# One Trainium2 core, Mamba-like block plus ternary FFN: another order for VectorE and ScalarE around the last three tiles, and the last block's norm on VectorE

## The chip, the cores and the metric

The kernel runs on one core of one Trainium2 chip. The metric is the device time of one execution in microseconds (us). The kernel before takes 1438.84 us, the median of 3 runs (1438.45 to 1439.49).

## What is computed

The input is 8192 rows of 512 numbers (float32). Two sublayers follow each other, each `x = x + norm(f(norm(x)))`, with `norm` a layer norm without weights:

```
uv = x @ in_proj_w + in_proj_b;  u, v = halves of uv;  v = silu(v)
v  = depthwise conv of 3 taps along the rows + conv_b
h_t = a * h_{t-1} + ssm_b * v_t;  y = ssm_c * h + ssm_d * v        (scan along the rows)
h  = (u * silu(y)) @ out_proj_w + out_proj_b + x
attn = layernorm(h) * ln_w + ln_b
ffn  = gelu(x @ ternary(W1).T + b1) @ ternary(W2).T + b2           (inner width 2048)
```

## The kernel before

**Tiles and stages.** The rows are cut into 16 tiles (`NT = 16`, numbered 0 to 15) of 512 rows, and each tile into 4 blocks of 128 rows. Wide products are made of float16 halves ("high" and "low", `hi` and `lo`), three matmuls for each pair, so each result of TensorE needs a low half made by VectorE. A tile goes through: its `v` and `u` products (`in_proj`, L498 to L500, 12 matmuls for each of 4 groups), the scan, the gate (`gate`, L847: bias and product of a finished `u` bank with silu(y)), the split of the gated tensor (`gate_hi`, ScalarE L1542; `gate_lo`, VectorE L852), the output product (`o`, L511 to L513, 12 matmuls for each of 4 blocks), the addition of its result to the residual (`h_add`, VectorE L871), three layer norms (`norms`, L891 to L915, with `a1`, `a2`, `b_stats`, `x1`, `c_stats`, `n3`), the split of the FFN's input (`t_hi`, ScalarE L1566; `t_lo`, VectorE L860), its transposes by DMA, and the FFN: 16 times `f1` (8 matmuls, L531, L532), `gelu` and `hi` on ScalarE (L1478, L1488), `lo` on VectorE (L754) and `f2` (8 matmuls, L559, L560), at the end the scaling and bias of the four sums (`f_add`, L767).

**The pipeline.** A step `s` handles three tiles at once: the FFN of tile `s-2`, the first sublayer of tile `s-1` and the first product of tile `s+1`; the end of tile `s-3` (its last norm and sum) lies in it too. The last steps are special. Step 15 has the second part of the FFN of tile 13 (chunks 9 to 15), then the `u` products and the output product of tile 15 behind them, since there is no further tile to load. Step 16 is the FFN of tile 14 with the norms of tile 15 beside it, step 17 the FFN of tile 15 alone, and then come the last norm and sum of tile 15.

**What sets the order.** Each engine works through its own list in order, and waits on semaphores. The lists are written out by hand, or sorted from tables of places (`AT_...` at the top): `run(items)` (L84) sorts pairs of a number and a piece of work. The numbers are places in the list, not times. `AT_LO_LAST` holds the places of `lo` of chunks 9 to 15 in step 15, `AT_LO` those of step 16, `AT_GATE_LAST` those of the first two gates of tile 15, `AT_T3_LO` those of `t_lo`. The norms of step 15 stand at 7.7 and each 0.25 further, those of step 16 at 0.5 and on. GpSimd (POOL) makes every reciprocal standard deviation: an addition (`ve`, L1865) and a power (L1866), and VectorE's `a1`, `x1` and `n3` wait for them. GpSimd also adds the output bias to the residual of tile 15 (`add_bias`, L1918, four of them) and makes the last sum of every tile but the last (`finish`, L1908).

**Banks.** `u`, `v` and `o` products take turns on two PSUM banks, `misc0` and `misc1`, so a product waits for the reader of the one two places before it: `u` group 2 of tile 15 waits for gate 0, group 3 for gate 1, `o` block 0 for gate 2, block 1 for gate 3, block 2 for `h_add` 0 and block 3 for `h_add` 1. `o` also waits for each `gate_lo`, quarter by quarter (L509). The FFN's sums of tile 13 lie in four banks `f2b`; `f_add` empties them, and may write block `j` of `hb` once `t_lo` of tile 14 has read that block.

**The end.** For tile 15 VectorE makes `f_add`, the statistics and their aggregate block by block (L1460). GpSimd makes scale and shift (`rstd_last`, L1899: `ve`, power, product, negation) for blocks 0 and 1 together, then 2, then 3 (`FINAL`, L67). ScalarE norms each block (`ffn_norm`, L1499), VectorE adds the residual (L1466, the residual less its own shift was made earlier by `less_shift`), and SyncE stores the block.

```
            for j in range(NB):
                ve_.wait_ge(fn_ok, NB * e + j + 1)
                ve_.tensor_tensor(hb[:, j, :], hb[:, j, :], xs[:, e % X_SLOTS, j, :], ALU.add).then_inc(fin_last, 1)
```

Of the kernel before, what the change touches and what calls it, by code (L numbers as in the profile page):

```python
# [28 lines left out]
KC = D // P  # L29
# [34 lines left out]
AT_SILU_LAST, AT_GATE_LAST = 16.15, (15.0, 15.75)  # L64
AT_LO_LAST = (8.6, 9.6, 10.6, 11.65, 11.66, 12.2, 12.9)
AT_T3_HI_PAIR = (16.2, 16.4, 16.6, 16.8)
AT_XC = 13.3  # L67
FINAL = ((0, 2), (2, 3), (3, 4))
# [24 lines left out]
def build(nc, x, w_in, w_out, w1t, w2t, params, rows, out):  # L93
# [22 lines left out]
    with ExitStack() as ctx:  # L116
# [603 lines left out]
        def _(ve_):  # L720
# [207 lines left out]

            def add_bias(j):

                ve_.wait_ge(row_in, 16)
                ve_.wait_ge(x1_lo, j + 1)
                ve_.tensor_tensor(hb[:, j, :], hb[:, j, :], ob_row, ALU.add).then_inc(ob_ok, 1)
# [437 lines left out]
            for s in STEPS:  # L1371
# [17 lines left out]
                if fa is not None:  # L1389
                    items += [(AT_LO[j] if j < len(AT_LO) else 1.2 + j, lambda j=j: lo(fa, j))  # L1390
                              for j in range(half(s))]
# [21 lines left out]
                if s == NT - 1:  # L1413
                    for b in range(KC):
                        taps(NT - 1, b, False)
                    scan(NT - 1, 0)
                    scan(NT - 1, 1)
                items = []
                if c is not None:
                    for j in range(NB):  # L1420
                        h_add(c, j)
                        if s == NT - 1:
                            if j < 2:
                                scan(NT - 1, 2 + j)
                            y(NT - 1, j)
# [11 lines left out]
                if c is not None:  # L1437
                    items += [(at, lambda j=j: t_lo("t3", c, j)) for j, at in enumerate(AT_T3_LO)]
# [3 lines left out]
                if s == NT - 1:  # L1442
# [6 lines left out]
                    for j in range(NB):  # L1449
                        f_add(NT - 3, j)  # L1450
                    for j in range(NB):
                        f_stats(NT - 3, j)
                        h_add(NT - 1, j)
# [10 lines left out]
            for j in range(NB):  # L1464
                ve_.wait_ge(fn_ok, NB * e + j + 1)
                ve_.tensor_tensor(hb[:, j, :], hb[:, j, :], xs[:, e % X_SLOTS, j, :], ALU.add).then_inc(fin_last, 1)  # L1466
# [3 lines left out]
        def _(act):  # L1470
# [323 lines left out]
            for s in STEPS:  # L1794
# [45 lines left out]
                if s == NT - 1:  # L1840
                    items += [(AT_SILU_LAST, lambda b=b: silu_y(NT - 1, b)) for b in range(KC)]
                run(items)
                if s == NT - 1:
                    for b in range(KC):
                        gate_hi(NT - 1, b)
            for i, (j0, j1) in enumerate(FINAL):
# [6 lines left out]
        def _(pool):  # L1853
# [45 lines left out]
            def rstd_last(js):  # L1899

                pool.wait_ge(fn_ok, NB * (NT - 1))
                rstd(4, NT - 1, rs4[:, js], False, js)
# [179 lines left out]
```

## Time and profile before

| | |
|---|---|
| runs | 1438.84 us median of 3 (1438.45 to 1439.49) |
| the profiled execution | 1439.29 us, of which the span from the first to the last instruction is 1436.6 us |
| TensorE (PE) busy | 1405.8 us, 98% of the span |
| VectorE (DVE) busy | 1116.4 us, 78% |
| ScalarE (ACT) busy | 876.9 us, 61% |
| GpSimd (POOL) busy | 437.0 us, 30% |
| granted TensorE clock | 0.995 of full speed |

The profile is of one execution. The rows of its views name an engine, a line of the kernel, the operation and the tensors written and read; a bracket at the end of a row of the timeline tells how long the engine was idle before it and what ended that. The busy shares are those of the whole span. The change touches only its last 200 us, so what it is worth is read from the timeline of that stretch.

### The profile page before, as it was taken

The numbers are of one execution on the slowest core, as the hardware profiler recorded it, in microseconds if no ns is written. First come the engines' busy times: TensorE is split into PE (matmuls) and PEld (weight loads), VectorE is DVE, ScalarE is ACT, GpSimd is POOL, SyncE is SP. The second block draws the span as 40 slices with busy tenths as digits, with TensorE's granted clock in tenths as the row PEclk, the third lists the DMA queues.
The fourth block names the chain that finished last, engine by engine and source line by source line (L and its number), as shares of the span: only waits on it lengthen the run. The fifth ranks groups of instructions, "written<-read, shape, count | busy, mean of one in ns | idle before, by whom it ended". The sixth has DMA issues, their size and how long they took to land.

```text
span 1436.6 us, 19033 instructions
## 1 busy us (share of the span) xinstructions
PE 1405.8 (98%) x6528; PEld 641.9 (45%) x6528; DVE 1116.4 (78%) x1891; ACT 876.9 (61%) x1261; POOL 437.0 (30%) x520
## 2 busy tenths in 40 slices
PE   7998999999999999999999999999999999999997
PEld 5443444444444444444444444444444444443443
DVE  7999796867878677796867978677786877998634
ACT  7897665656756466565656756466565656753443
POOL 4325142320513225132330424214132331522221
PEclk9999999999999999999999999999999999999999
DMA  9713211221213113111221213113121221001200
GB/s 249 240 40 90 57 60 30 61 57 31 67 23 89 30 30 88 27 62 30 55 64 30 67 23 88 30 30 88 22 68 30 52 66 30 30 1 30 59 30 29
DMA packets 155984, 82.00 MB, mean 57 GB/s; under 512 B 132720, under 2 KB 132720, under 8 KB 155760
## 3 DMA queue, kind: packets, MB, share of 16 engines
q1 hardware_dynamic: 155888, 80.79, 22.0%
q8 instruction: 51, 0.84, 0.2%
q14 instruction: 45, 0.37, 0.1%
HBM read 31.49 MB, written 16.78 MB: 34 GB/s over the span
## 4 chain that ended last, share of the span: by engine, by line
PE 83%; DVE 4%; issue 2%; ACT 1%; POOL 1%; DMA 0%; DVEq 0%; POOLq 0%; ACTq 0%; SPq 0%
PE f1b L531 14%; PE f1b L532 14%; PE f2b L559 14%; PE f2b L560 14%; PE misc L498 6%; PE misc L500 6%; PE misc L499 6%; PE misc L511 3%; PE misc L513 3%; PE misc L512 3%; DVE bn L736 1%; DVE vl L812 0%; DVE yb L847 0%; DVE g_lo L852 0%; POOL rsc L1866 0%
## 5 line engine op out<-in xcount | busy, mean ns | idle before, releaser
L559 PE MATMUL f2b<-w,ring 128*128 128x512 fp8e5 x1008 | 382.1, 379 | 0.6 <-DVE ring L754 0.6
L560 PE MATMUL f2b<-w,ring 128*128 128x512 fp8e5 x1008 | 382.0, 379 | 0.0
L531 PE MATMUL f1b<-x3T,w 128*128 128x512 f16 x960 | 365.0, 380 | 2.3 <-DMA x3T<-tp 0.9
L532 PE MATMUL f1b<-x3T,w 128*128 128x512 f16 x960 | 365.0, 380 | 0.0
L1478 ACT ACTIVATE ring<-f1b,par 128x512 f32<-128x512 f32 x256 | 175.1, 684 | 238.9 <-PE f1b L532 238.5
L1865 POOL TENSOR_SCALAR ve<-mv 128x4 f32<-128x4 f32 (+2 forms) x88 | 33.6, 382 | 718.7 <-DVE mv L746 718.5
L754 DVE SCALAR_TENSOR_TENSOR ring<-ring,f_sc 128x512 f16<-128x512 f32 x256 | 208.7, 829 | 41.0 <-ACT ring L1488 41.0
L1488 ACT ACTIVATE ring<-ring,f_sc 128x512 f16<-128x512 f32 x256 | 180.0, 711 | 0.0
L498 PE MATMUL misc<-x1T,win_hi 128*128 128x512 f16 x464 | 175.9, 379 | 2.2 <-DVE yb L847 2.1
L500 PE MATMUL misc<-x1T,win_lo 128*128 128x512 f16 x464 | 175.9, 379 | 0.0
L499 PE MATMUL misc<-x1T,win_hi 128*128 128x512 f16 x464 | 175.9, 379 | 0.0
L559 PEld LDWEIGHTS f2b<-w,ring 128*128 128x128 f16 x1008 | 98.6, 98 | 120.4 <-DVE ring L754 1.9
L560 PEld LDWEIGHTS f2b<-w,ring 128*128 128x128 f16 x1008 | 98.6, 98 | 118.5
L531 PEld LDWEIGHTS f1b<-x3T,w 128*128 128x128 fp8e5 x960 | 94.1, 98 | 118.0 <-issue 4.9
L532 PEld LDWEIGHTS f1b<-x3T,w 128*128 128x128 fp8e5 x960 | 94.1, 98 | 113.4 <-issue 1.3
L1591 ACT ACTIVATE vb<-misc,par,inv_sig 128x512 f32<-128x512 f32 x54 | 41.8, 775 | 143.7 <-PE misc L500 143.6
L736 DVE BATCH_NORM_STATS2 bn<-hb 128x6 f32<-128x512 f32 x184 | 118.9, 679 | 0.2
L812 DVE SCALAR_TENSOR_TENSOR vl<-vb,par,vl 128x512 f32<-128x512 f32 x128 | 108.2, 883 | 1.8 <-ACT vl L1508 1.7
L1908 POOL TENSOR_TENSOR hb<-hb,xs 128x512 f32<-128x512 f32 x60 | 102.2, 1733 | 21.8 <-ACT hb L1499 21.8
L1918 POOL TENSOR_TENSOR hb<-hb,row 128x512 f32<-128x512 f32 x56 | 73.7, 1318 | 86.4 <-ACT hb L1529 86.4
L511 PE MATMUL misc<-wo_hi,g_hi 128*128 128x512 f16 x240 | 91.0, 379 | 4.9 <-DVE hb L871 2.8
L1913 POOL COPY carry<-vl 128x1 f32<-128x1 f32 x60 | 73.0, 1233 | 63.0 <-DVE vl L821 61.9
(211 smaller groups left out, 2043.1 us busy)
## 6 DMA issues: line engine op xcount, KB each, us to landing
out_dram<-hb SPq DMA_DIRECT2D x64, 256.0 KB, 2.0
xs<-x_dram SPq DMA_DIRECT2D x14, 1024.0 KB, 5.7
ring<-w1t_dram SPq DMA_DIRECT2D x3, 1024.0 KB, 12.3
stage<-w2t_dram SPq DMA_DIRECT2D x3, 1024.0 KB, 8.2
x1T<-tp SPq DMA_TRANSPOSE x68, 3.1
xs<-x_dram SPq DMA_DIRECT2D x4, 256.0 KB, 3.4
stage<-w_in_dram SPq DMA_DIRECT2D x4, 256.0 KB, 5.6
xs<-x_dram SPq DMA_DIRECT2D x2, 512.0 KB, 7.2
```

The lines of the kernel that those rows point to most:

```text
L498: pe.matmul(o[:, :], wh, x1T[:, s_, k, :], start=k == 0, stop=False)
L499: pe.matmul(o[:, :], wh, x1T[:, s_, KC + k, :], start=False, stop=False)
L500: mm = pe.matmul(o[:, :], wl, x1T[:, s_, k, :], start=False, stop=k == KC - 1)
L511: pe.matmul(out_[:, :], g_hi[:, k, js], wo_hi[:, k, :], start=k == 0, stop=False)
L531: pe.matmul(b[:, :], w, src[:, k, :], start=k == 0, stop=False)
L532: mm = pe.matmul(b[:, :], w, src[:, KC + k, :], start=False, stop=k == KC - 1)
L559: pe.matmul(f2b[q][:, :], h_hi[:, i % H_SLOTS, qs], w2[:, j, :], start=j == 0, stop=False)
L560: mm = pe.matmul(f2b[q][:, :], h_lo[:, i % H_SLOTS, qs], w2[:, j, :], start=False, stop=j == FC - 1)
L736: ve_.bn_stats(raw_stats(ln)[:, j, :], src).then_inc(bn_ok[ln], 1)
L754: ve_.scalar_tensor_tensor(out=h_lo[:, i % H_SLOTS, :], in0=gg[:, i % G_SLOTS, :], scalar=f_sc[:, 0:1], in1=h_hi[:, i % H_SLOTS, :], op0=A ...
L1478: act.activation(gg[:, i % G_SLOTS, :], f1b[i % 2][:, :], ACT.Gelu, bias=par[:, B1 + j:B1 + j + 1], scale=1.0 / ACT_SCALE).then_inc(gelu_o ...
L1488: act.activation(h_hi[:, i % H_SLOTS, :], gg[:, i % G_SLOTS, :], ACT.Copy, scale=f_sc[:, 0:1]).then_inc(hh_ok, 1)
```

## The change

- In step 15 the first `lo` (chunk 9) goes ahead of the four `a1`, and behind them no `lo` stands any more until the four `a2` are through.
- In step 15 scan 1 of tile 15 goes behind the first `h_add` of tile 14, scans 2 and 3 each one place later too.
- Gate 1 of tile 15 goes from behind the first two `t_lo` to right behind gate 0; `t_lo` of blocks 2 and 3 of tile 14 go behind the last `gate_lo`. ScalarE makes `gate_hi` 0 and 1 between `t_hi` 1 and 2.
- The first `h_add` of tile 15 goes between the second and third `f_add` of tile 13, the others one place forward among the statistics.
- In step 16 the places of the first eight `lo` are others (`AT_LO_PAIR`).
- The last block of tile 15 is normed by VectorE from mean and scale; ScalarE no longer does it, and GpSimd's product and negation for it are gone.

```diff
-AT_SILU_LAST, AT_GATE_LAST = 16.15, (15.0, 15.75)
-AT_LO_LAST = (8.6, 9.6, 10.6, 11.65, 11.66, 12.2, 12.9)
+AT_SILU_LAST, AT_GATE_LAST, AT_GATE_HI_LAST = 16.15, (15.0, 15.1), 16.5
+AT_LO_LAST = (7.65, 9.6, 10.6, 11.65, 11.66, 12.2, 12.9)
...
+AT_LO_PAIR = (0.45, 1.3, 1.9, 2.4, 3.4, 5.1, 6.0, 7.3)
...
+            def last_norm(j):
+
+                ve_.wait_ge(rs_ok[4], NT + len(FINAL) - 1)
+                ve_.tensor_scalar(hb[:, j, :], hb[:, j, :], mean_var(4)[:, j, 0:1], rs4[:, j:j + 1],
+                                  ALU.subtract, ALU.mult).then_inc(fn_ok, 1)
+
+            def last_sum(j):
+
+                ve_.wait_ge(fn_ok, NB * (NT - 1) + j + 1)
+                ve_.tensor_tensor(hb[:, j, :], hb[:, j, :], xs[:, (NT - 1) % X_SLOTS, j, :], ALU.add).then_inc(fin_last, 1)
...
-                    items += [(AT_LO[j] if j < len(AT_LO) else 1.2 + j, lambda j=j: lo(fa, j))
+                    at_lo = AT_LO_PAIR if s == NT else AT_LO
+                    items += [(at_lo[j] if j < len(at_lo) else 1.2 + j, lambda j=j: lo(fa, j))
...
                     scan(NT - 1, 0)
-                    scan(NT - 1, 1)
...
                         if s == NT - 1:
-                            if j < 2:
-                                scan(NT - 1, 2 + j)
+                            if j < NB - 1:
+                                scan(NT - 1, 1 + j)
                             y(NT - 1, j)
...
-                    items += [(at, lambda j=j: t_lo("t3", c, j)) for j, at in enumerate(AT_T3_LO)]
+                    items += [(at, lambda j=j: t_lo("t3", c, j)) for j, at in enumerate(AT_T3_LO) if s < NT - 1 or j < 2]
...
-                    for j in range(NB):
-                        f_add(NT - 3, j)
+                    t_lo("t3", NT - 2, 2)
+                    t_lo("t3", NT - 2, 3)
+                    f_add(NT - 3, 0)
+                    f_add(NT - 3, 1)
+                    h_add(NT - 1, 0)
+                    f_add(NT - 3, 2)
+                    f_add(NT - 3, 3)
                     for j in range(NB):
                         f_stats(NT - 3, j)
-                        h_add(NT - 1, j)
+                        if j < NB - 1:
+                            h_add(NT - 1, j + 1)
                         h_stats(NT - 1, j)
                         aggr(4, NT - 3, j)
...
-            for j in range(NB):
-                ve_.wait_ge(fn_ok, NB * e + j + 1)
-                ve_.tensor_tensor(hb[:, j, :], hb[:, j, :], xs[:, e % X_SLOTS, j, :], ALU.add).then_inc(fin_last, 1)
+            for j in range(NB - 1):
+                last_sum(j)
+            last_norm(NB - 1)
+            last_sum(NB - 1)
...
                     items += [(AT_SILU_LAST, lambda b=b: silu_y(NT - 1, b)) for b in range(KC)]
+                    items += [(AT_GATE_HI_LAST, lambda b=b: gate_hi(NT - 1, b)) for b in range(2)]
                 run(items)
                 if s == NT - 1:
-                    for b in range(KC):
+                    for b in range(2, KC):
                         gate_hi(NT - 1, b)
-            for i, (j0, j1) in enumerate(FINAL):
+            for i, (j0, j1) in enumerate(FINAL[:-1]):
...
                 pool.wait_ge(fn_ok, NB * (NT - 1))
+                if js.stop == NB:
+                    rstd(4, NT - 1, rs4[:, js], True, js)
+                    return
```

Three pieces of VectorE's list show what moved, as lines with the operation and its tensors; a line of the changed kernel has a number higher by one. The first is the beginning of the norms of tile 14 in step 15. L891 is `a1`, L896 `a2`, and the write to `ring` is `lo` of chunks 9 and 10. Before:

```order
L746 BN_AGGR mv<-bn 128x2 x2
L891 SCALAR_TENSOR_TENSOR hb<-hb,mv,row 128x512 x4
L754 SCALAR_TENSOR_TENSOR ring<-ring,f_sc 128x512
L896 SCALAR_TENSOR_TENSOR hb<-hb,rsc,row 128x512 x4
L754 SCALAR_TENSOR_TENSOR ring<-ring,f_sc 128x512
```

Now:

```order
L747 BN_AGGR mv<-bn 128x2 x2
L755 SCALAR_TENSOR_TENSOR ring<-ring,f_sc 128x512
L892 SCALAR_TENSOR_TENSOR hb<-hb,mv,row 128x512 x4
L897 SCALAR_TENSOR_TENSOR hb<-hb,rsc,row 128x512 x4
L755 SCALAR_TENSOR_TENSOR ring<-ring,f_sc 128x512
```

`lo` of chunk 9 went from behind the `a1` to ahead of them, and nothing stands between `a1` and `a2`.

The second piece is the end of these norms. `hb<-xs,mv,rsc` is `n3`, `yb<-misc...` a gate, `tp<-hb,tp` is `t_lo` and `g_lo` is `gate_lo`. Before:

```order
L915 TENSOR_SCALAR hb<-xs,mv,rsc 128x512 x2
L847 SCALAR_TENSOR_TENSOR yb<-misc0,bu_sig,yb 128x512
L915 TENSOR_SCALAR hb<-xs,mv,rsc 128x512
L860 SCALAR_TENSOR_TENSOR tp<-hb,tp 128x512
L915 TENSOR_SCALAR hb<-xs,mv,rsc 128x512
L860 SCALAR_TENSOR_TENSOR tp<-hb,tp 128x512
L847 SCALAR_TENSOR_TENSOR yb<-misc1,bu_sig,yb 128x512
L860 SCALAR_TENSOR_TENSOR tp<-hb,tp 128x512 x2
L852 SCALAR_TENSOR_TENSOR g_lo<-yb,g_sc,g_hi 128x512
L847 SCALAR_TENSOR_TENSOR yb<-misc0,bu_sig,yb 128x512
```

Now:

```order
L916 TENSOR_SCALAR hb<-xs,mv,rsc 128x512 x2
L848 SCALAR_TENSOR_TENSOR yb<-misc0,bu_sig,yb 128x512
L848 SCALAR_TENSOR_TENSOR yb<-misc1,bu_sig,yb 128x512
L916 TENSOR_SCALAR hb<-xs,mv,rsc 128x512
L861 SCALAR_TENSOR_TENSOR tp<-hb,tp 128x512
L916 TENSOR_SCALAR hb<-xs,mv,rsc 128x512
L861 SCALAR_TENSOR_TENSOR tp<-hb,tp 128x512
L853 SCALAR_TENSOR_TENSOR g_lo<-yb,g_sc,g_hi 128x512
L848 SCALAR_TENSOR_TENSOR yb<-misc0,bu_sig,yb 128x512
```

Gate 1 (the first on `misc1`) has moved over an `n3` and a `t_lo` and more, and the last two `t_lo` are gone from ahead of the first `gate_lo`.

The third piece follows it: `hb<-f2b...` is `f_add` of tile 13 and `xs<-misc...` is `h_add` of tile 15. Before:

```order
L852 SCALAR_TENSOR_TENSOR g_lo<-yb,g_sc,g_hi 128x512
L847 SCALAR_TENSOR_TENSOR yb<-misc1,bu_sig,yb 128x512
L852 SCALAR_TENSOR_TENSOR g_lo<-yb,g_sc,g_hi 128x512 x2
L767 SCALAR_TENSOR_TENSOR hb<-f2b0,f_inv,row 128x512
L767 SCALAR_TENSOR_TENSOR hb<-f2b1,f_inv,row 128x512
L767 SCALAR_TENSOR_TENSOR hb<-f2b2,f_inv,row 128x512
L767 SCALAR_TENSOR_TENSOR hb<-f2b3,f_inv,row 128x512
L736 BN_STATS bn<-hb 128x6
L871 SCALAR_TENSOR_TENSOR xs<-misc0,o_inv,xs 128x512
```

Now:

```order
L853 SCALAR_TENSOR_TENSOR g_lo<-yb,g_sc,g_hi 128x512
L848 SCALAR_TENSOR_TENSOR yb<-misc1,bu_sig,yb 128x512
L853 SCALAR_TENSOR_TENSOR g_lo<-yb,g_sc,g_hi 128x512 x2
L861 SCALAR_TENSOR_TENSOR tp<-hb,tp 128x512 x2
L768 SCALAR_TENSOR_TENSOR hb<-f2b0,f_inv,row 128x512
L768 SCALAR_TENSOR_TENSOR hb<-f2b1,f_inv,row 128x512
L872 SCALAR_TENSOR_TENSOR xs<-misc0,o_inv,xs 128x512
```

The two `t_lo` stand here now, behind all four `gate_lo`, and `h_add` 0 has gone ahead of two `f_add` and a `bn_stats`.

## Rows read from the trace of the kernel before

**Rows 1.** The page: busy time, share of the span, instructions of each engine

```profile
PE 1405.8 (98%) x6528; PEld 641.9 (45%) x6528; DVE 1116.4 (78%) x1891; ACT 876.9 (61%) x1261; POOL 437.0 (30%) x520
```

**Rows 2.** Timeline of TensorE, end of step 15: start us, us, row, [idle <-what ended it]

```profile
1263.84 0.39 PE L511 MATMUL misc<-wo_hi,g_hi 128*128 128x512 f16 x1 [0.20 <-DVE hb L871]
...
1278.40 0.39 PE L559 MATMUL f2b<-w,ring 128*128 128x512 fp8e5 x1 [0.58 <-DVE ring L754]
...
1298.91 0.38 PE L500 MATMUL misc<-x1T,win_lo 128*128 128x512 f16 x1
...
1303.45 0.39 PE L498 MATMUL misc<-x1T,win_hi 128*128 128x512 f16 x1 [1.39 <-DVE yb L847]
...
1308.84 0.39 PE L511 MATMUL misc<-wo_hi,g_hi 128*128 128x512 f16 x1
...
1312.72 0.39 PE L511 MATMUL misc<-wo_hi,g_hi 128*128 128x512 f16 x1 [0.48 <-DVE xs L871]
```

**Rows 3.** Timeline of VectorE, scans, additions and norms of tile 14, step 15

```profile
1261.88 1.25 DVE L821 TENSOR_TENSOR_SCAN vl<-a_par,carry,vl 128x512 f32<-128x512 f32 x1
1263.06 0.72 DVE L871 SCALAR_TENSOR_TENSOR hb<-misc,o_inv,hb 128x512 f32<-128x512 f32 x1
...
1274.94 2.74 DVE L891 SCALAR_TENSOR_TENSOR hb<-hb,mv,row 128x512 f32<-128x512 f32 x4 [1.47 <-POOL rsc L1866]
1277.60 0.74 DVE L754 SCALAR_TENSOR_TENSOR ring<-ring,f_sc 128x512 f16<-128x512 f32 x1
...
1284.90 1.38 DVE L754 SCALAR_TENSOR_TENSOR ring<-ring,f_sc 128x512 f16<-128x512 f32 x2
...
1291.41 0.73 DVE L754 SCALAR_TENSOR_TENSOR ring<-ring,f_sc 128x512 f16<-128x512 f32 x1
```

**Rows 4.** Timeline of GpSimd, step 15: powers for the norms, last bias addition

```profile
1273.87 1.04 POOL L1866 TENSOR_TENSOR rsc<-ve,mhalf 128x4 f32<-128x4 f32 x1
...
1285.79 1.39 POOL L1866 TENSOR_TENSOR rsc<-ve,mhalf 128x4 f32<-128x4 f32 x1
...
1299.67 1.45 POOL L1918 TENSOR_TENSOR xs<-xs,row 128x512 f32<-128x512 f32 x1
```

**Rows 5.** Timeline of VectorE, end of step 15: n3, t_lo and the first f_add

```profile
1295.68 2.89 DVE L915 TENSOR_SCALAR hb<-xs,mv,rsc 128x512 f32<-128x512 f32 x2 [1.47 <-POOL rsc L1866]
...
1299.91 1.75 DVE L860 SCALAR_TENSOR_TENSOR tp<-hb,tp 128x512 f16<-128x512 f32 x1
...
1303.31 1.28 DVE L860 SCALAR_TENSOR_TENSOR tp<-hb,tp 128x512 f16<-128x512 f32 x2
...
1308.69 2.72 DVE L767 SCALAR_TENSOR_TENSOR hb<-f2b,f_inv,row 128x512 f32<-128x512 f32 x4
```

**Rows 6.** Timeline of ScalarE, the last high half of the gated tensor

```profile
1307.27 0.72 ACT L1542 ACTIVATE g_hi<-yb,g_sc 128x512 f16<-128x512 f32 x1 [0.60 <-DVE yb L847]
```

**Rows 7.** Timeline of VectorE and TensorE, step 16: x1, lo and f2 of chunk 5

```profile
1338.58 2.74 DVE L906 SCALAR_TENSOR_TENSOR xs<-xs,rsc 128x512 f32<-128x512 f32 x4 [3.68 <-POOL c L1889]
...
1343.02 0.74 DVE L754 SCALAR_TENSOR_TENSOR ring<-ring,f_sc 128x512 f16<-128x512 f32 x1
...
1343.60 0.38 PE L532 MATMUL f1b<-x1T,w 128*128 128x512 f16 x1
1343.82 0.39 PE L559 MATMUL f2b<-w,ring 128*128 128x512 fp8e5 x1
```

**Rows 8.** Timeline of the end: VectorE, ScalarE, GpSimd

```profile
1430.25 1.88 DVE L1466 TENSOR_TENSOR hb<-hb,xs 128x512 f32<-128x512 f32 x3
1433.43 0.69 DVE L1466 TENSOR_TENSOR hb<-hb,xs 128x512 f32<-128x512 f32 x1 [1.30 <-ACT hb L1499]
...
1432.59 0.81 ACT L1499 ACTIVATE hb<-hb,nm,rs 128x512 f32<-128x512 f32 x1 [1.48 <-POOL nm L1904]
...
1431.08 0.88 POOL L1866 TENSOR_TENSOR rs<-ve,mhalf 128x1 f32<-128x1 f32 x1
```

**Rows 9.** n3 on tile 15 with GpSimd idle (line L915): ns min/median/max

```profile
L915 DVE TENSOR_SCALAR xs<-xs,mv,rsc x4: 539/540/546, 1346.8 to 1348.8; 128x512 f32<-128x512 f32 x4
```

## The prediction

> **What bounds the kernel now.** The page first [rows 1]: TensorE is busy 98% of the span, the next engine 78%. So outside the start and the end only what makes TensorE wait can be won back. The timeline of TensorE in the stretch that the change touches comes second [rows 2]. A matmul is modelled as 0.38 us long, but the next starts 0.22 us after it (the two TensorE rows of [rows 7]), so a wait costs its bracket and 0.16 us more. The reader is to see four larger ones: 0.36 us before 1263.84 (for `h_add` of tile 14), 0.74 before 1278.40 (for `lo` of chunk 9), 1.55 before 1303.45 (for gate 1 of tile 15) and 0.64 before 1312.72 (for `h_add` 0 of tile 15). All four end on VectorE. The third view is VectorE's own timeline there [rows 3, 5], for what stands ahead of the piece that TensorE wants. The last is the end [rows 8]: after the sums of the last block GpSimd makes the power, a product and a negation, ScalarE norms, VectorE adds.
>
> What is won in step 15 stays won only if nothing later pins TensorE at a fixed time, so each step is followed to the next wait.
>
> **Scans (step 15).** Scan 1 starts at 1261.88 and `h_add` 0 follows it at 1263.06 [rows 3]. Now `h_add` 0 takes the earlier place, 1.18 us before, and the 0.36 us go. VectorE's own total is unchanged: its norms still start when they did.
>
> **First `lo` ahead of `a1`.** Before, VectorE is idle for 1.47 us ahead of the `a1` [rows 3], waiting for the power, which runs 1273.87 to 1274.91 [rows 4]. `lo` of chunk 9 (about 0.66 us from start to start: `a1` four times take 1274.94 to 1277.60) moves into that idle time. TensorE's wait of 0.74 us goes. VectorE would gain 0.66 us for all that follows, if `lo` in the gap cost the power nothing. Rows 4 speak against that: the second power has two `lo` beside it (the row at 1284.90 of [rows 3]) and takes 1.39 instead of 1.04 us, 0.35 more. One `lo` beside `ve` and power can cost nothing at best, and at worst its whole 0.66 us. I take 0.40, near the only row that shows such an overlap. The norms then run 0.26 us earlier (bounds 0 and 0.66).
>
> TensorE has by then won 0.36 + 0.74 = 1.10 us, but gets no further than VectorE: `lo` of chunk 10 stands behind all four `a2`, and `lo` of chunk 15 ends at 1292.14 [rows 3], where TensorE takes it up with hardly any wait before. Both run 0.26 us earlier, so here TensorE's gain shrinks from 1.10 to 0.26 us. **Most of the first two waits comes back as waits for `lo` 10 and `lo` 15.**
>
> **Gates and `t_lo`.** The two first `n3` start at 1295.42 (1295.68 less 0.26) and end after 2.89 us [rows 5], at 1298.31; gate 0 follows. Gate 1 needs `u` group 1, whose last matmul started at 1298.91 [rows 2]; 0.26 earlier and 0.42 for its end gives 1299.07. It ends at 1299.8, and TensorE, which starts group 2 at about 1299.0 and needs 12 matmuls of 0.216 us for it, reaches group 3 at 1301.6 without a wait: the 1.55 us go.
>
> Then VectorE: the third `n3` comes at 1299.7, during GpSimd's last addition, which now runs 1299.4 to 1300.9 (1299.67 and 1.45 us, less 0.26 [rows 4]). In the trace before, a `t_lo` that starts during that addition takes 1.75 us and ends 0.54 us behind it [rows 4, 5]; so I let the `n3` end at 1301.2. Behind it, by 0.6 for a `t_lo` (two take 1.28, the first's end lying under the second [rows 5]), 0.46 for an `n3` and 0.66 for gates and `gate_lo`: `t_lo` 0, `n3` 3, `t_lo` 1 until 1302.8; `gate_lo` 0 at 1302.8, gate 2 at 1303.46, `gate_lo` 1 at 1304.12, gate 3 at 1304.78, `gate_lo` 2 at 1305.44. Gate 3 ends at 1305.52; ScalarE's high half takes 0.72 [rows 6] and ends at 1306.28; `gate_lo` 3 runs 1306.32 to 1307.06, and TensorE starts the last quarter of `o` block 0 at 1307.12, where it was 1308.84 [rows 2]: **1.72 us earlier**. It still waits ahead of the last two quarters, about as long as before, since 1.2 us of `t_lo` are out of the way but TensorE is there sooner too.
>
> `h_add` 0: `gate_lo` 3, two `t_lo` (1.2) and two `f_add` (1.32, by four in 2.64) give its start at 1309.5 and its end at 1310.24. TensorE, with 15 more matmuls from 1307.12, needs it at 1310.36. So the 0.64 us go too, and TensorE enters step 16 **2.36 us earlier**. `h_add` 1 ends at 1312.8, needed at 1312.95: just in time.
>
> `f_add` 2 and 3 end later than the first two but are wanted only by `f2` of tile 14, five `f1` after the start of step 16: nothing. `t_lo` 2 and 3 end at 1308.2, their transposes are wanted 7 us later: nothing.
>
> **Step 16.** TensorE had no waits here and is now 2.36 us earlier at every chunk, and the new places answer that. The tightest is `lo` 5: it ended at 1343.76 and was wanted at 1343.82 [rows 7]. In its new place, behind three `x1`, it ends 2.0 + 0.75 us behind the start of the first. That start hangs on GpSimd, whose additions follow TensorE's time, so 1338.58 becomes 1336.2 and `lo` 5 ends at 1339.0; wanted at 1341.46. Nothing lost, so the 2.36 us reach the end.
>
> **The last block.** The power ends at 1431.96; from there a product, a negation, ScalarE's 0.81 us and 0.69 us of addition end at 1434.12 [rows 8]. Now VectorE norms itself: free after its three additions at about 1432.05 (start 1430.25, 0.60 each), 0.54 us for `n3`'s form with GpSimd idle [rows 9], then the addition from 1432.62. That replaces 1433.43: **0.81 us**. Bounds: 0.3 if this form took as long as ScalarE's 0.81 and the wait between the two were longer than between VectorE's others, 0.9 if VectorE were free at the power's end.
>
> **Sum.** 2.36 + 0.81 = 3.17 us off the profiled execution (1439.29, span 1436.6): 1436.1, span 1433.4. That execution is 0.45 us above the median of the runs. The median is forecast at 1438.84 - 3.17 = 1435.7 us. A measurement of this kernel can tell about 0.2%, 2.9 us, from no change, so the forecast lies 0.3 us beyond that line.
>
> **The rivals.**
> 1. *GpSimd has the port when `lo` 9 starts.* `lo` 9 starts at about 1273.64, while GpSimd is in the addition ahead of the power. If it blocks, or the power is pushed back by all of it, VectorE has nothing for all that follows: 2.36 - 0.26 + 0.81 = 2.91 us, 1435.9. For it: `t_lo` of 1.75 us [rows 5]. Against it: the power with two `lo` beside it lost only 0.35 us. The Trainium skill (SBUF — State Buffer, Who interferes with whom) says that whichever of VectorE with two SBUF inputs and GpSimd issues first holds the shared pair for its whole instruction and the other fully blocks; that is this rival, its sum would be 1435.9. By that rule the `t_lo` of 1.75 us agrees, and the power's 0.35 us, less than one `lo`, does not quite.
> 2. *No contention at all:* the norms run 0.66 earlier, 2.76 + 0.81 = 3.57 us, 1435.3. For it: one small instruction of GpSimd may slip by.
> 3. *TensorE finds a new wait:* `h_add` 1 has 0.15 us to spare, `h_add` 0 has 0.12, the quarters of `o` wait on VectorE in any case. If VectorE loses 1 us more (say that `n3` and `t_lo` both wait out GpSimd's additions), all of it shows: 2.17 us or less in all, 1436.7. With the last block's norm worth only 0.3 as well, 1.66 us, 1437.2.
> 4. *Slower: `lo` 5 is pinned behind `x1`.* `x1` waits for GpSimd, busy with four additions beside a VectorE without pause; 3.68 us of idle ahead of it [rows 7] show that this wait is real. `lo` 5 has 2.5 us to spare. Each us beyond costs TensorE one; at 5.6 us later the gain is gone, and from 8.5 us the kernel is slower by 0.2%: at 10 us, 1443.1. Against it: nothing added to GpSimd's work there.
>
> **Chances.** Forecast 0.45, rival 1 0.21, rival 2 0.13, rival 3 0.18, rival 4 0.03. The forecast and rival 1 lie near the line of 2.9 us (1435.96), so with a spread of the median of some 0.3 us I count three quarters of the first (0.34) and half of the second (0.11) as beyond it, and all of rival 2: 0.58 faster, 0.39 the same, 0.03 slower. The range takes in rivals 1 to 3 with their bounds and that spread: 1434.8 to 1437.2.
>
> **What would show it.** After: no bracket ahead of `u` group 3; the first `lo` inside VectorE's idle time ahead of `a1`, with the second part of that idle time telling whether the power grew; a wait of TensorE for `lo` 10 (`f2`), new; the last quarter of `o` block 0 about 1.7 us earlier; no wait for `h_add`; no waits in steps 16 and 17; the last addition 0.57 us behind VectorE's norm. The forecast is wrong if TensorE enters step 16 less than 2 or more than 2.8 us earlier, or if steps 16 and 17 have waits.

## The result and the profile after

The changed kernel takes 1436.07 us (median of 20 runs, 1433.88 to 1439.53), the kernel before beside it on the same chip 1438.53 us (20 runs, 1437.32 to 1442.02). The ratio is 0.9981, 95% interval 0.9975 to 0.9988: 2.7 us gone, 1.7 to 3.6 by the interval. The forecast was 1435.7 us and 3.17 us. The effect is real, since the interval leaves out no change. But its middle, 2.7 us, lies just short of the 2.9 us (0.2%) beyond which the prediction had put 0.58 of its chances.

The profiled execution of after has a span of 1436.6 us, the same as before's. It must not be read as "nothing gained". Two rows show why: the first `u` matmul of tile 14, the start of step 15. Everything ahead of it is unchanged code.

Timeline of TensorE, kernel before (start us, us, engine line op out<-in count [idle <-what ended it], so in all timelines below):

```profile
1241.02 0.38 PE L498 MATMUL misc<-x1T,win_hi 128*128 128x512 f16 x1
```

The same place, kernel after (its lines are numbered one higher here):

```profile
1243.76 0.38 PE L499 MATMUL misc<-x1T,win_hi 128*128 128x512 f16 x1
```

This execution reached step 15 2.74 us later. Single executions of one kernel lie 2 us and more to each side of their median, so neither spans nor single times settle an effect of 2.7 us. What repeats to some 0.02 us is the waits of TensorE inside one trace. So I use this measure: over all matmuls from 1225 us on, the sum of (start to start less 0.216 us) wherever the distance is over 0.25 us. It is 4.30 us in before and 2.36 in after: 1.94 us won. (The sums are of unrounded starts; those of printed rows can be 0.02 off.) The rest is the end: from the start of the last matmul to the end of the last addition 5.90 us before, 5.09 after, so 0.81 us. Together 2.75 us, which agrees with the ratio.

Page, after, busy time of each engine ([rows 1] of before):

```profile
PE 1406.8 (98%) x6528; PEld 641.7 (45%) x6528; DVE 1119.3 (78%) x1892; ACT 876.6 (61%) x1260; POOL 435.3 (30%) x518
```

VectorE has one instruction more, and 2.9 us more busy time, most of which is no work, as its rows in step 16 below show.

Timeline of TensorE, after, its six waits ([rows 2]; subtract 2.74 us to compare starts; the bracket leaves out 0.16 us, and waits below it have none):

```profile
1284.16 0.39 PE L560 MATMUL f2b<-w,ring 128*128 128x512 fp8e5 x1 [0.53 <-DVE ring L755]
...
1294.64 0.39 PE L560 MATMUL f2b<-w,ring 128*128 128x512 fp8e5 x1
...
1301.74 0.39 PE L499 MATMUL misc<-x1T,win_hi 128*128 128x512 f16 x1
...
1308.68 0.39 PE L512 MATMUL misc<-wo_hi,g_hi 128*128 128x512 f16 x1 [0.30 <-DVE g_lo L853]
...
1309.56 0.39 PE L512 MATMUL misc<-wo_hi,g_hi 128*128 128x512 f16 x1
...
1344.59 0.39 PE L560 MATMUL f2b<-w,ring 128*128 128x512 fp8e5 x1 [0.53 <-DVE ring L755]
```

In order: 0.69 us for `lo` 10 and 0.11 for `lo` 15 (new), 0.18 for gate 0, 0.45 and 0.22 for the last two `gate_lo` (0.60 and 0.23 before), and 0.69 for `lo` 5 of step 16 (new). The waits for `h_add`, `lo` 9 and gate 1 of [rows 2] are gone. Before step 16 the sum is 1.66 us, so TensorE entered it 4.30 - 1.66 = 2.64 us earlier. In step 16 it gave 0.69 back.

Timeline of VectorE and GpSimd, after, step 15, around `lo` 9 ([rows 3, 4]):

```profile
1276.37 0.75 DVE L755 SCALAR_TENSOR_TENSOR ring<-ring,f_sc 128x512 f16<-128x512 f32 x1
1278.05 2.74 DVE L892 SCALAR_TENSOR_TENSOR hb<-hb,mv,row 128x512 f32<-128x512 f32 x4 [0.93 <-POOL rsc L1886]
...
1276.63 1.39 POOL L1886 TENSOR_TENSOR rsc<-ve,mhalf 128x4 f32<-128x4 f32 x1
```

`lo` 9 lies in the idle time, and the power beside it takes 1.39 us instead of 1.04: `a1` starts 0.35 us later than it could. The forecast had taken 0.40.

Timeline of VectorE and GpSimd, after, step 16 (L897 is `a2`, L755 `lo`, L907 `x1`; L1931 are the four additions of `finish`):

```profile
1328.60 2.42 DVE L897 SCALAR_TENSOR_TENSOR xs<-xs,rsc,row 128x512 f32<-128x512 f32 x2
1330.95 1.75 DVE L755 SCALAR_TENSOR_TENSOR ring<-ring,f_sc 128x512 f16<-128x512 f32 x1
1332.62 3.43 DVE L897 SCALAR_TENSOR_TENSOR xs<-xs,rsc,row 128x512 f32<-128x512 f32 x2
1335.98 0.74 DVE L755 SCALAR_TENSOR_TENSOR ring<-ring,f_sc 128x512 f16<-128x512 f32 x1
...
1341.79 2.08 DVE L907 SCALAR_TENSOR_TENSOR xs<-xs,rsc 128x512 f32<-128x512 f32 x3 [1.75 <-POOL c L1909]
1343.79 0.74 DVE L755 SCALAR_TENSOR_TENSOR ring<-ring,f_sc 128x512 f16<-128x512 f32 x1
...
1328.90 3.25 POOL L1931 TENSOR_TENSOR hb<-hb,xs 128x512 f32<-128x512 f32 x2 [3.65 <-ACT hb L1518]
1332.36 3.15 POOL L1931 TENSOR_TENSOR hb<-hb,xs 128x512 f32<-128x512 f32 x2 [0.20 <-ACT hb L1518]
1340.13 0.23 POOL L1885 TENSOR_SCALAR ve<-mv 128x4 f32<-128x4 f32 x1 [4.62 <-DVE mv L747]
```

Two engines alternate here. The second `a2` starts 0.67 us behind the first, at 1329.27, and from there to 1335.98 VectorE issues four instructions in 6.71 us, 1.68 each instead of 0.66: 4.1 us lost, one for each addition of GpSimd. The `x1` then start at 1341.79, and `lo` 5 behind three of them ends 0.69 us late. Note the last row: GpSimd is idle for 4.62 us and waits for VectorE, not the other way round.

Before, the same four additions cost VectorE nothing. Timeline of GpSimd and VectorE, before, the first addition and what VectorE did beside it, and in the last row GpSimd's first instruction behind the fourth addition:

```profile
1328.83 3.88 POOL L1908 TENSOR_TENSOR hb<-hb,xs 128x512 f32<-128x512 f32 x1 [5.33 <-ACT hb L1499]
...
1328.84 0.75 DVE L754 SCALAR_TENSOR_TENSOR ring<-ring,f_sc 128x512 f16<-128x512 f32 x1
1329.50 0.75 DVE L896 SCALAR_TENSOR_TENSOR xs<-xs,rsc,row 128x512 f32<-128x512 f32 x1
1330.16 1.41 DVE L754 SCALAR_TENSOR_TENSOR ring<-ring,f_sc 128x512 f16<-128x512 f32 x2
1331.49 2.47 DVE L736 BATCH_NORM_STATS2 bn<-xs 128x6 f32<-128x512 f32 x4
...
1336.92 0.23 POOL L1865 TENSOR_SCALAR ve<-mv 128x4 f32<-128x4 f32 x1
```

Here GpSimd was held for 3.88 us, to 1.13 us behind the end of the last of VectorE's instructions with two SBUF inputs (1331.57), and VectorE kept its pace. The last row is the `ve` that `x1` waits for: it starts as the fourth addition ends, so in before `x1` hung on GpSimd's additions, as the prediction says, and in after on VectorE's statistics. GpSimd's bias additions of the same shape take 1.32 us in the mean. The lines view of GpSimd, before (op count | busy, mean ns | idle ahead):

```profile
L1918 POOL TENSOR_TENSOR hb<-hb,row 128x512 f32<-128x512 f32 x56 | 73.7, 1318 | 86.4 <-ACT hb L1529 86.4
```

The meeting itself had moved. Timeline of VectorE, before, the first three `a1` of step 16:

```profile
1323.53 2.08 DVE L891 SCALAR_TENSOR_TENSOR xs<-xs,mv,row 128x512 f32<-128x512 f32 x3 [3.59 <-POOL rsc L1866]
```

Timeline of GpSimd and VectorE, after, ahead of `a1` in step 16:

```profile
1323.17 0.65 POOL L1917 TENSOR_SCALAR nm<-tmp 128x4 f32<-128x4 f32 x1
...
1322.97 0.75 DVE L755 SCALAR_TENSOR_TENSOR ring<-ring,f_sc 128x512 f16<-128x512 f32 x1 [1.70 <-ACT ring L1507]
1325.28 1.42 DVE L892 SCALAR_TENSOR_TENSOR xs<-xs,mv,row 128x512 f32<-128x512 f32 x2 [1.56 <-POOL rsc L1886]
```

`a1` started at 1323.53 in before and at 1325.28 - 2.74 = 1322.54 in after: only 0.99 us earlier, since the statistics behind the last `f_add` were ready only 1.4 us earlier and one small GpSimd instruction took 0.65 us beside a `lo`, where it took 0.24 in before. The additions follow TensorE: 1328.90 - 2.74 = 1326.16, 2.67 us earlier. So they fall 1.7 us sooner into VectorE's norms.

Timeline of the end, after ([rows 8]; L933 is the norm, L939 the addition, L1886 the power):

```profile
1431.02 1.87 DVE L939 TENSOR_TENSOR hb<-hb,xs 128x512 f32<-128x512 f32 x3
1432.81 0.54 DVE L933 TENSOR_SCALAR hb<-hb,mv,rs 128x512 f32<-128x512 f32 x1
1433.39 0.69 DVE L939 TENSOR_TENSOR hb<-hb,xs 128x512 f32<-128x512 f32 x1
...
1431.85 0.88 POOL L1886 TENSOR_TENSOR rs<-ve,mhalf 128x1 f32<-128x1 f32 x1
```

Product, negation and ScalarE's pass are gone; the addition follows the norm by 0.58 us.

### The profile page after: what moved, and what is told of

Read it like the earlier page. It is cut to its first block, busy times and chain, and to the rows that moved or that the text cites. A ratio compares the mean times of both kernels' runs of the same rounds, so it can differ in the third digit from the quotient of the medians.

```text
span 1436.6 us, 19031 instructions
## 1 busy us (share of the span) xinstructions
PE 1406.8 (98%) x6528; PEld 641.7 (45%) x6528; DVE 1119.3 (78%) x1892; ACT 876.6 (61%) x1260; POOL 435.3 (30%) x518
## 4 chain that ended last, share of the span: by engine, by line
PE 77%; DVE 7%; issue 4%; ACT 1%; POOL 1%; DMA 1%; SPq 0%; DVEq 0%; ACTq 0%; POOLq 0%
PE f1b L532 13%; PE f2b L560 13%; PE f1b L533 13%; PE f2b L561 13%; PE misc L499 6%; PE misc L501 6%; PE misc L500 6%; PE misc L512 3%; PE misc L514 3%; PE misc L513 3%; DVE bn L737 1%; POOL rsc L1886 1%; DMA x3T<-tp 1%; DVE ring L755 1%; DVE hb L892 1%
## 5 line engine op out<-in xcount | busy, mean ns | idle before, releaser
L755 DVE SCALAR_TENSOR_TENSOR ring<-ring,f_sc 128x512 f16<-128x512 f32 x256 | 208.4, 827 | 40.8 <-ACT ring L1507 40.7
L1931 POOL TENSOR_TENSOR hb<-hb,xs 128x512 f32<-128x512 f32 x60 | 100.7, 1707 | 20.7 <-ACT hb L1518 20.7
```

The source lines that it names most:

```text
L755: ve_.scalar_tensor_tensor(out=h_lo[:, i % H_SLOTS, :], in0=gg[:, i % G_SLOTS, :], scalar=f_sc[:, 0:1], in1=h_hi[:, i % H_SLOTS, :], op0=A ...
```

## The experiments

Two theories stood after the result. **A:** the wait for `lo` 5 comes from the contention of VectorE and GpSimd in step 16, the alternation above. **B:** it comes from the new place of `lo` 5 alone. Beside them each part of the change was to be priced by itself. "Waits" is the measure above (before 4.30, after 2.36 us). Where a kernel was timed only once, its time is given beside that of the kernel before, but the waits decide. A short diff is against the changed kernel, unless it says otherwise.

### The end alone, and the changed kernel again

The first is the kernel before with `last_norm` and `last_sum`, and GpSimd's and ScalarE's parts of the last block left out. The second is unchanged.

```diff
# e1_end_only, against before
-            for j in range(NB):
-                ve_.wait_ge(fn_ok, NB * e + j + 1)
-                ve_.tensor_tensor(hb[:, j, :], hb[:, j, :], ...)
+            for j in range(NB - 1):
+                last_sum(j)
+            last_norm(NB - 1)
+            last_sum(NB - 1)
```

> The kernel before with the last block normed by VectorE and nothing else. If the term of the last block is right: from the start of the last matmul to the end of the last addition 5.90 us before, now 5.09 us (0.81 less), with the norm of 0.54 us starting when VectorE's third addition is through; TensorE's waits after 1240 us stay at 4.29 us in all. Rival (ScalarE's hand-over was hidden): 5.6 us or more.

> The changed kernel again. In its first profile TensorE waits 0.69 us for lo 5 of step 16, because four VectorE instructions of the norms there took 1.75 us instead of 0.75 beside GpSimd's additions (4.1 us lost). If that is how this order always meets GpSimd: the same four long instructions, TensorE's waits after 1240 us 2.3 to 2.4 us. If it is a matter of chance who gets there first: in this run VectorE's instructions are short, GpSimd's first addition takes 3 us or more, no wait for lo 5, 1.65 us in all.

The end alone: waits 4.31, last matmul to end 5.09 instead of 5.90 (one time, 1436.93, beside 1438.24). So the last part is worth 0.81 us by itself, and the two parts add. GpSimd's first addition in step 16 takes 3.88 us in this run too. The changed kernel again (1436.17 beside 1438.24): waits 2.35, among them 0.68 for `lo` 5, and the alternation is there to the hundredth.

VectorE, changed kernel again, step 16:

```profile
1326.06 2.42 DVE L897 SCALAR_TENSOR_TENSOR xs<-xs,rsc,row 128x512 f32<-128x512 f32 x2
1328.40 1.75 DVE L755 SCALAR_TENSOR_TENSOR ring<-ring,f_sc 128x512 f16<-128x512 f32 x1
1330.08 3.43 DVE L897 SCALAR_TENSOR_TENSOR xs<-xs,rsc,row 128x512 f32<-128x512 f32 x2
```

So which engine gives way is no chance of one execution; it repeats with the order. The alternation of the additions stands in every run with the changed places of step 16 and the additions ahead of the norms' work.

### `lo` 5 ahead of `x1`

```diff
-AT_LO_PAIR = (0.45, 1.3, 1.9, 2.4, 3.4, 5.1, 6.0, 7.3)
+AT_LO_PAIR = (0.45, 1.3, 1.9, 2.4, 3.4, 4.4, 6.0, 7.3)
```

> The changed kernel with lo 5 of step 16 ahead of x1 (4.4 instead of 5.1), into VectorE's idle time. Theory: the wait of 0.69 us for it goes, TensorE's waits after 1240 us 1.65 us, and the kernel is 3.4 us faster than before (ratio 0.9976); lo 6 then ends within 0.1 us of its need. Rival (lo 6 and 7 are as late, the wait only moves to the next chunk): waits stay at 2.3 us.

Waits 1.74: `lo` 5 is waited for no more, 0.07 us come back for `lo` 6. The alternation stays (2.42, 1.75, 3.43 us). Timed: 1436.66 us (11 runs) beside 1438.24 (15), ratio 0.999 (0.998 to 0.9999); too wide to show 0.6 us. Both theories allow this one: the place turns the loss of VectorE into a wait of TensorE.

### The additions of `finish` behind GpSimd's norm work

```diff
-                if e is not None:
+                if e is not None and s != NT:
                     items += [(0, lambda j=j: finish(e, j)) for j in range(NB)]
...
                     rstd(3, c, rsc[:, 2, :], True)
+                if s == NT:
+                    for j in range(NB):
+                        finish(e, j)
```

> The changed kernel with GpSimd's four additions for tile 13 moved behind its work for the norms of tile 15. Theory: the four VectorE instructions of 1.75 us in step 16 take 0.75 again, everything from the a2 on is 4.1 us earlier, lo 5 is in time, TensorE's waits after 1240 us are 1.65 us. Rival (something else holds x1): the wait of 0.69 us stays.

Timeline of VectorE in this run, step 16:

```profile
1324.41 1.41 DVE L897 SCALAR_TENSOR_TENSOR xs<-xs,rsc,row 128x512 f32<-128x512 f32 x2
1325.73 0.74 DVE L755 SCALAR_TENSOR_TENSOR ring<-ring,f_sc 128x512 f16<-128x512 f32 x1
1326.40 1.40 DVE L897 SCALAR_TENSOR_TENSOR xs<-xs,rsc,row 128x512 f32<-128x512 f32 x2
...
1342.14 5.70 DVE L916 TENSOR_SCALAR xs<-xs,mv,rsc 128x512 f32<-128x512 f32 x4 [1.24 <-POOL rsc L1886]
```

`lo` 5 kept its place behind `x1`, and its wait is gone: waits 1.67 (1435.33 beside 1438.11). That decides for A: the place costs nothing if VectorE isn't slowed. The contention moved to the four `n3`, 5.70 us, where four of 0.54 us [rows 9] would take 2.2 at most; nobody waits for them.

### The old places of `lo` in step 16

```diff
-                    at_lo = AT_LO_PAIR if s == NT else AT_LO
+                    at_lo = AT_LO
```

> The changed kernel with the old places of lo in step 16. Theory: TensorE, 2.6 us earlier than in the kernel before, outruns them: it waits about 1 us for lo 0 (behind three a1), and for lo 5 (behind all x1 and three statistics) 1 us or more; waits after 1240 us 3.5 us or more. Rival (the places buy nothing, only the contention of VectorE and GpSimd decides): 2.4 us as in the changed kernel.

Waits 5.04 us: 1.11 for `lo` 0, 1.79 for `lo` 1, 0.45 for `lo` 5 (1441.22 beside 1438.11). TensorE enters the step 2.64 us earlier than in before, `a1` starts only 1.4 us earlier (0.99 in after, where a `lo` stands beside GpSimd's chain), and a `lo` that stood in time behind it is now late. VectorE gives way to the additions here too (single instructions of 1.75 us), so it is not the new order of `lo` alone that turned the contest. The table of places is what keeps the gain of step 15: 2.68 us of it, the largest single price measured here. Without it the waits are longer than the 4.30 us of before.

### `lo` 9 back behind `a1`

```diff
-AT_LO_LAST = (7.65, 9.6, 10.6, 11.65, 11.66, 12.2, 12.9)
+AT_LO_LAST = (8.6, 9.6, 10.6, 11.65, 11.66, 12.2, 12.9)
```

> The changed kernel with lo 9 of step 15 behind the a1 again. Theory (lo 9 beside GpSimd's power costs 0.35 and frees 0.66): the power takes 1.04 instead of 1.39 us, the a1 start 0.35 us earlier against the aggregates, but everything from the a2 on is 0.31 us later; TensorE waits about 1.1 us for lo 9, nothing for lo 10, and enters step 16 0.3 us later than the changed kernel. Rival (no cost, 0.66 freed): 0.66 us later. Rival (all given back): at the same time.

Waits 2.68, 0.32 more (1439.39 beside 1438.24). TensorE waits 1.14 us for `lo` 9, but not for `lo` 10 (0.69) nor `lo` 15 (0.11). The power takes 1.04 us again. So most of this wait had only changed its name, as forecast.

### Gate 1 back

```diff
-AT_SILU_LAST, AT_GATE_LAST, AT_GATE_HI_LAST = 16.15, (15.0, 15.1), 16.5
+AT_SILU_LAST, AT_GATE_LAST, AT_GATE_HI_LAST = 16.15, (15.0, 15.75), 16.5
```

> The changed kernel with gate 1 of tile 15 back behind two n3 and two t_lo. Theory: TensorE waits 1.5 us for it again, the last quarter of o block 0 starts 1.6 us later than in the changed kernel; as TensorE then comes later to lo 5, that wait goes: waits after 1240 us 3.2 to 4.0 us. Rival (VectorE's total up to the last gate_lo decides, gate 1's place is worth little): 2.4 to 2.8 us.

Waits 3.89: 1.54 for gate 1 again, all else as in after (1435.89 beside 1438.11). The wait for `lo` 5 stayed at 0.70, although TensorE was 1.54 us later; I had thought that it might go. The additions and the norms follow TensorE, so all of them moved together. The gate is the change's main gain, and worth its whole wait.

### Scan 1 back ahead of `h_add` 0

```diff
                     scan(NT - 1, 0)
+                    scan(NT - 1, 1)
...
-                            if j < NB - 1:
-                                scan(NT - 1, 1 + j)
+                            if j < 2:
+                                scan(NT - 1, 2 + j)
```

> The changed kernel with scan 1 ahead of the first h_add of tile 14, as before. Theory (what the scan frees comes back as a wait for lo 10): the wait of 0.37 us for h_add returns and that for lo 10 shrinks from 0.69 to 0.32, the sum stays 2.36 us. Rival (the scan's gain is real): 2.7 us.

A miss, and the most useful run. Waits 1.99 (1436.95 beside 1438.11): *less* than the changed kernel's 2.36. The 0.37 us for `h_add` are back, but the 0.69 for `lo` 10 are gone. Timeline of VectorE and GpSimd, this run:

```profile
1275.33 0.75 DVE L755 SCALAR_TENSOR_TENSOR ring<-ring,f_sc 128x512 f16<-128x512 f32 x1 [0.53 <-ACT ring L1508]
1276.27 2.74 DVE L892 SCALAR_TENSOR_TENSOR hb<-hb,mv,row 128x512 f32<-128x512 f32 x4 [0.19 <-POOL rsc L1887]
...
1275.20 1.04 POOL L1887 TENSOR_TENSOR rsc<-ve,mhalf 128x4 f32<-128x4 f32 x1
```

TensorE is 0.37 us later here, so ScalarE gives `lo` 9 its input later. It starts 0.13 us *behind* the power and slows nothing; in after it starts 0.26 us *ahead* of it and costs it 0.35. `a1` is then 0.36 us earlier against the norms and TensorE 0.37 later: together 0.73, enough for the 0.69.

The Trainium skill (SBUF — State Buffer, Who interferes with whom) says that of a VectorE instruction with two SBUF inputs and a GpSimd instruction that reads SBUF the one that issues first holds the shared port pair and the other fully blocks. In the pair of runs here the order of the starts does decide, as it says. In after `lo` still had 0.49 us to run when the power began, and the power lost 0.35. But in e8 the power began first and neither blocked, which the rule does not give.

### Both: scan back, additions late

```diff
# e9_scan_back_finish_late: the two edits above together
```

> The changed kernel with two things of the runs before: scan 1 ahead of the first h_add again, and GpSimd's additions for tile 13 behind its work for the norms of tile 15. If the two are independent: TensorE's waits after 1240 us 1.99 - 0.69 = 1.30 us, the end 5.09 us behind the last matmul, together 3.8 us less than the kernel before, ratio 0.9973. Rival (what one frees meets the next wait): 1.7 to 2 us.

Waits 1.32 against 1.30 expected: the two causes are independent. Timed: 1435.15 us (12 runs) beside 1439.21 (23), ratio 0.9976 (0.9965 to 0.9987).

### Gates between the `n3`, `o` blocks interleaved

```diff
# against e9, VectorE
+                    late_n3[0]()
+                    gate(NT - 1, 0)
+                    late_n3[1]()
+                    gate(NT - 1, 1)
                     gate_lo(NT - 1, 0)
...
                     gate_lo(NT - 1, 3)
+                    late_n3[2]()
+                    t_lo("t3", NT - 2, 0)
+                    late_n3[3]()
+                    h_add(NT - 1, 0)
+                    t_lo("t3", NT - 2, 1)
...
+                    h_add(NT - 1, 1)
+                    for j in range(NB):
+                        f_add(NT - 3, j)
...
# TensorE
+                    o_part(first, 0, range(KC - 1))
+                    o_part(second, 1, range(1))
+                    o_part(first, 0, range(KC - 1, KC))
+                    o_part(second, 1, range(1, KC))
```

ScalarE makes its four high halves of the gate before the last two of `x3`.

> The same, and at the end of step 15 VectorE makes only two n3 ahead of the gates (gate 0 between them), the other n3 and all t_lo behind the last gate_lo, and TensorE makes the last quarter of o block 0 behind the first of block 1. Theory: the waits for gate 0 (0.17) and for the last two gate_lo (0.46 and 0.22) go, the chain gate 3, high half, gate_lo 3 of 2.5 us lying beside 12 matmuls now; waits after 1240 us 0.5 us, 4.6 us less than before, ratio 0.9968. Rival (h_add 0 and 1, now behind n3 and t_lo, are late): 1 us or more.

A miss. Waits 1.84, timed 1436.32 (11 runs) beside 1439.21 (23), ratio 0.9981 (0.9972 to 0.999). Timeline of TensorE and of SP's queue, this run:

```profile
1305.77 0.39 PE L522 MATMUL misc<-wo_hi,g_hi 128*128 128x512 f16 x1 [0.28 <-DVE g_lo L870]
...
1315.80 0.38 PE L543 MATMUL f1b<-x1T,w 128*128 128x512 f16 x1 [0.79 <-DMA x1T<-tp]
...
1307.73 5.99 SPq L405 DMA_TRANSPOSE x1T<-tp  x4
```

The gates' waits shrank from 0.85 to 0.44 us, but all of `t_lo` came behind them, the transposes with it, and `f1` of step 16 waited 0.95 us for the last. The prediction's "wanted 7 us later: nothing" for the transposes held for the change, but it left out that SP issues them one after the other: the four take 5.99 us together, of which 0.43 is a wait for a `t_lo`. With the last `t_lo` 2.2 us later than in after, the margin is gone.

### The same, with `n3` and `t_lo` spread between the gates

```diff
# against e10, VectorE
                     gate_lo(NT - 1, 0)
+                    late_n3[2]()
                     gate(NT - 1, 2)
                     gate_lo(NT - 1, 1)
-                    gate(NT - 1, 3)
+                    t_lo("t3", NT - 2, 0)
                     gate_lo(NT - 1, 2)
+                    gate(NT - 1, 3)
+                    t_lo("t3", NT - 2, 1)
                     gate_lo(NT - 1, 3)
-                    late_n3[2]()
-                    t_lo("t3", NT - 2, 0)
                     late_n3[3]()
-                    h_add(NT - 1, 0)
-                    t_lo("t3", NT - 2, 1)
                     t_lo("t3", NT - 2, 2)
+                    h_add(NT - 1, 0)
```

ScalarE's third high half of `x3` moves ahead of its third one of the gate.

> The run before showed two waits: 0.44 us for gate_lo 2, which stood behind gate 3 on VectorE, and 0.95 us for the transposes of tile 14, whose last t_lo ended at 1310.6. Now gate_lo 2 goes ahead of gate 3, and the n3 and t_lo fill VectorE's idle time between the gates. Theory: both waits go, what is left is 0.37 + 0.07, TensorE's waits after 1240 us 0.45 to 0.65 us, ratio to the kernel before 0.9968. Rival (a gate or gate_lo is pushed back by what was put ahead of it): 0.9 us or more.

Waits 0.78: 0.37 for `h_add`, 0.07 for `lo` 15, and 0.35 for `lo` 1 of step 16, the next to be late (below). Between `lo` 15 and step 16 there is no wait left. Timed: 1435.15 us (9 runs) beside 1438.63 (13), ratio 0.9975 (0.9965 to 0.9985).

Timeline of TensorE, VectorE and GpSimd, this run:

```profile
1326.35 0.39 PE L571 MATMUL f2b<-w,ring 128*128 128x512 fp8e5 x1 [0.18 <-DVE ring L772]
...
1322.89 2.74 DVE L909 SCALAR_TENSOR_TENSOR xs<-xs,mv,row 128x512 f32<-128x512 f32 x4 [3.24 <-POOL rsc L1912]
1325.55 0.74 DVE L772 SCALAR_TENSOR_TENSOR ring<-ring,f_sc 128x512 f16<-128x512 f32 x1
...
1318.89 0.75 DVE L772 SCALAR_TENSOR_TENSOR ring<-ring,f_sc 128x512 f16<-128x512 f32 x1
...
1319.14 1.41 POOL L1912 TENSOR_TENSOR rs<-ve,mhalf 128x4 f32<-128x4 f32 x1
```

Here `lo` 1 stands behind four `a1`, as `lo` 10 stands behind the four `a2` in after. The last two rows show `lo` 0 once more 0.25 us ahead of a power of the chain that `a1` waits for, and the power at 1.41 us instead of 1.04; that loss is as large as the wait, but no run tried `lo` 0 at another place. By the waits this is the best version, 1.58 us under the changed kernel; by time it can't be told from the e9 kernel, and it was not timed beside the changed kernel itself. Both beat the kernel before with their intervals.

## Why the prediction was right, and where it was not

| term | forecast, us | measured, us | from |
|---|---|---|---|
| TensorE enters step 16 earlier | 2.36 | 2.64 | waits 4.30 and 1.66 |
| step 16 | nothing lost | 0.69 lost | new wait for `lo` 5 |
| last block | 0.81 | 0.81 | 5.90 and 5.09 |
| sum | 3.17 | 2.76 (2.75 unrounded) | ratio: 2.7 |

**Scans.** The wait for `h_add` went, 0.37 us. In the forecast's sum this was worth nothing, since it lies in the 1.10 us that shrink to 0.26. That it cost nothing either was wrong: the run with the scan back shows that it brought `lo` 9 ahead of the power and cost more than it gave (1.99 against 2.36 us). The prediction priced the two parts of the change one by one and did not carry the 0.37 us of TensorE on to the start of `lo` 9.

**First `lo` ahead of `a1`.** Right in mechanism and size: power 0.35 us longer (taken 0.40), norms 0.3 earlier (0.26), the first two waits back as waits for `lo` 10 and 15 (0.69 and 0.11 seen). The run with `lo` 9 back confirms it. Rivals 1 and 2, the norms no earlier or a whole 0.66 us earlier, are both excluded for this kernel. Rival 1 had priced a block at the whole `lo`; 0.49 us of it were left when the power began.

**Gates and `t_lo`.** Right: gate 1's wait gone, priced at 1.54 us by the run with it back. The last quarter of `o` block 0 started at 1309.56, less 2.74 that is 1306.82: 2.02 us earlier, where 1.72 was forecast. Of the 0.30 us 0.27 are VectorE's third `n3`: it ended at 1300.93 on before's clock, not 1301.2, since GpSimd's four bias additions were done 0.26 us sooner. No wait for `h_add` 0 or 1.

Timeline of VectorE and GpSimd, after, the third `n3` and the bias additions ([rows 4, 5]):

```profile
1302.50 1.17 DVE L916 TENSOR_SCALAR hb<-xs,mv,rsc 128x512 f32<-128x512 f32 x1
...
1298.06 5.32 POOL L1941 TENSOR_TENSOR xs<-xs,row 128x512 f32<-128x512 f32 x4
```

The additions end at 1303.38, less 2.74 that is 1300.64, where the forecast had 1300.9.

**Step 16: the step that failed.** "Nothing lost" rested on two sentences: that GpSimd's additions follow TensorE's time, so that the `x1` start at 1336.2, and that `lo` 5 had 2.5 us to spare. The additions did follow. But the `x1` started at 1341.79, less 2.74 that is 1339.05: not 2.4 us earlier than before but 0.5 later, and 2.85 later than forecast. VectorE lost 4.1 us to the additions, and `x1` waited for its statistics, no longer for GpSimd: on before's clock the additions ended 4.2 us earlier than in before. The 2.85 us less `lo` 5's spare time, 2.46, which TensorE's extra 0.28 cut to 2.18, are 0.67; 0.69 was measured. The trace of before has an addition of 3.88 us there, three times the usual; that row was not read, and it was the sign that two engines contend there. What VectorE loses when it is the one that gives way stood in the prediction's own rows: two `n3` in 2.89 us and a `t_lo` of 1.75 beside the bias additions [rows 5]. It was counted in step 15 and left out in step 16. Rival 4 named the right instruction and the right pin but the wrong holder (a busy GpSimd); the delay was 2.85 us, far from the 8.5 at which it would have decided.

**Last block.** Right to 0.01 us, in the change and alone.

So the time fell into the range because a loss of 0.69 us and a gain of 0.28 both were smaller than the rivals allowed for. That 0.28 us of the loss were made up in step 15 is luck. By the prediction's own sign, waits in steps 16 and 17, its account of step 16 was wrong. What stays open: why GpSimd is shut out in before and alternates in after. It was not tried in isolation.

## What to carry to other kernels

When a step is moved earlier, follow its own timing to each place where VectorE and GpSimd overlap, and read the longest instance of a GpSimd instruction, not its mean: one that is three times its usual length marked, here, a contest that a shift of 1.7 us turned. An earlier TensorE is worth only what the vector work in the next stage can follow, so the places of that work belong to the change (here 2.68 us of it). Where runs scatter by more than the effect, sum TensorE's waits within one trace and undo each part of the change by itself: a part that removes a wait can still cost time.

## What the runs showed of the hardware

- Four GpSimd additions of 128x512 beside VectorE's instructions with two SBUF inputs went in two ways, each the same in every run of the same order. In before and in the kernel with only the end changed, the first was held for 3.88 us while VectorE kept 0.66 us per instruction. In the changed kernel both runs show strict alternation, VectorE at 1.68 us per instruction and GpSimd at 1.6 per addition. The 3.88 us stand alone: of the 120 GpSimd instructions of 128x512 with two inputs in before, the next longest took 2.29 us.
- In the alternation each engine waits for the other in full, up to a hand-over. An addition that found VectorE in such an instruction ended 1.13 us behind the end of that one, 0.14 less than its usual 1.27 us (56 of the 120 in before took that). A VectorE instruction of 0.75 us that waited for an addition ended 0.55 us behind its end, 0.20 less. 1.13 and 0.55 are the 1.68 us of a pair. The addition of 3.88 us too ended 1.13 us behind the last of the four VectorE instructions that went ahead of it.
- That agrees with the rule of the Trainium skill from above. What does not is that four VectorE instructions with later starts went ahead of the waiting addition.
- The starts that go with the two ways differ by little. The first addition started 0.01 us ahead of a VectorE instruction in before, and 0.30 us behind one in after. With the old places of `lo` it started 0.06 us behind an `a2`, which led to alternation. The second pair of additions in that run started 0.05 us ahead of a `lo`, and two `lo` took 3.44 us together (the rows below). So whether GpSimd gets in may turn on differences under 0.1 us; that was not tried by itself, and these starts do not order all cases. Timeline of VectorE and GpSimd, run with the old places of `lo`:

```profile
1333.33 3.44 DVE L755 SCALAR_TENSOR_TENSOR ring<-ring,f_sc 128x512 f16<-128x512 f32 x2
...
1333.28 2.94 POOL L1931 TENSOR_TENSOR hb<-hb,xs 128x512 f32<-128x512 f32 x2 [1.09 <-ACT hb L1518]
```

- VectorE's `n3`, which reads one tensor, gives way to the additions as well (four in 5.70 us with the additions late). The statistics, 0.68 us each in before, and a gate, which reads one of its two tensors from PSUM, 0.74 us, were not slowed beside an addition.
- A power on 128x4 took 1.39 us where a `lo` had begun 0.26 us ahead of it: 0.35 more, which is the 0.49 that `lo` had left, less 0.14 again. It took 1.04 us where the `lo` began 0.13 us behind it, with the `lo` at 0.75 us in both. So one overlap of a VectorE instruction with two SBUF inputs and a small GpSimd instruction cost neither engine anything.
